# A fused decoder layer on one core: GpSimd places a step's queries ahead, TensorE turns the maxima alone

## The chip, the cores and the metric

The kernel runs on one core of one Trainium2 chip. The metric is the device time of one execution in microseconds (us). The profile calls the engines PE (TensorE matmuls), PEld (TensorE weight loads), DVE (VectorE), ACT (ScalarE), POOL (GpSimd) and SP (SyncE, whose queue issues the DMAs here).

## What is computed

The reference is one decoder layer on x of shape (8, 128, 128), that is 8 batch entries of 128 tokens of width 128. It has three parts, each on the layer norm of x and added back to x:

```python
x = x + attn(layernorm(x), ...)      # self attention, 16 heads of 8, scores * tau + delta, softmax
x = x + xattn(layernorm(x), ctx)     # cross attention, 16 heads of 8, masked, softmax
x = x + ffn(layernorm(x), ...)       # 64 experts, top 4 of 8 groups, top 8 experts, and a shared one
# in both attentions
scores = einsum('bhqd,bhkd->bhqk', Q, K) / sqrt(8)
attn   = softmax(scores);  out = einsum('bhqk,bhkd->bhqd', attn, V)
```

## The kernel before

The kernel is one program with its engines' instruction streams written out by hand; semaphores order them. After a start-up that makes queries and keys (to about 43 us of the profile) come 16 attention steps, s = 0 to 15: one batch entry each, the first 8 of the self attention (n = 0), the last 8 of the cross attention (n = 1). Then the experts' part runs in units to the end.

Queries and keys are kept "stacked". `qst` holds, for each of G = 4 groups of 4 heads, a band of 32 rows for each head: 8 rows that take the maxima, then the parts of the head's query. `kst` is the same for the keys. `scores(s, g)` on PE multiplies `qst` with the diagonal blocks of keys `kbd` (four matmuls in a step, one for each group; with a mask matmul before each from s = 8 on). DVE takes the row maxima of each (`maximum`, L1129), and `split_max` (L1136, L1137) writes them, as a high and a low part, to `negmax`.

`turn_max(s)` on PE then fills bank 5 with two matmuls: L521 copies the stacked queries of the step into it (identity times `qst`), and L524 adds the turned maxima. `queries_with_max(s)` copies the four bands of bank 5 to the four diagonal blocks of `qbd`, in the half `s % 2`: ACT two of them (L896), DVE the other two (L1145), 32 rows of 512 elements each. `scoresT(s, g)` on PE multiplies `kst` with `qbd`, which gives the transposed scores with the maximum taken off already; ACT takes the exponential (L887), `pv` multiplies with the values, `copy_o`, `turn_out`, `norm`, `turn_on`, `copy_on`, `project` and `add_residual` finish the step, each by its engine and partly one or two steps later.

In one round of the loop, PE runs `scores(s+1, 0)`, `turn_max(s)`, `scores(s+1, 1)`, `project(s-2)`, `pv(s-1)` with `scores(s+1, 2)` in its middle, `scoresT(s, 0)` and `(s, 1)`, `scores(s+1, 3)`, `turn_out(s-1)`, `scoresT(s, 2)` and `(s, 3)`, `turn_on(s-1)`. DVE runs `split_max(s)`, `maximum(s+1, 0)`, `queries_with_max(s)`, `maximum(s+1, 1)`, `add_residual(s-2)`, `maximum(s+1, 2)` and `(s+1, 3)`, `norm(s-1)`. In rounds 7 and 11 half of the cross attention's queries is made between: on ACT `queries_with_max(s)` and then the bias copy L942 to `qhl`, on DVE L1312, then the stacking matmuls on PE and the copies to `qst` by ACT (L922) and DVE (L1279, `second_stacked`); only after those can `scores(s+1, ...)` run. They need the layer norm of the first or last four entries, `second_inputs`, at the end of rounds 6 and 10. In rounds 2 and 3 `values(1, c)` of the cross attention are made as well.

POOL has little to do in these steps: after memsets it scales the values (L1421), makes `sel` (L1426, L1427) after step 0, and runs `normalise` (L263 to L277: some 15 tiny linked operations, then four of 128x128 into `xn`) and `add_bias` (L283) for each half, when `stats_ready` says that the residuals of its four entries are done. It then splits the first three expert weights (L1451 to L1455, L1444), normalises the first half for the experts (last `xn` at 154 us) and goes on to `low_inputs(0)` (L1437) and the second half. A POOL operation that is given to `link` is followed by a wait for its own completion.

Of the kernel before, what the change touches and what calls it, by code (L numbers as in the profile page):

```python
# [11 lines left out]
ALU = mybir.AluOpType  # L12
# [3 lines left out]
P = 128  # L16
B = 8
T = B * P
H, DK = 16, 8
G = 4  # L20
J = H // G
HALF = T // 2
E, I = 64, 64
# [5 lines left out]
STEPS = 2 * B  # L29
S_HI, S_MID, S_LO = 2 * G, 2 * G + DK, 2 * G + 2 * DK  # L30
PER_HALF = PAIRS + 1
UNITS = 2 * PER_HALF
LAG = 3
# [25 lines left out]
def decoder_layer(nc, x, ctxT, mask, pack_a, pack_b, w3, rowsd, outT):  # L59
# [3 lines left out]
    with ExitStack() as ctx:  # L63
# [3 lines left out]
        def sem(name):  # L67
            return ctx.enter_context(nc.semaphore(name))

        bank = [ctx.enter_context(nc.psum_tensor(f"bank{i}", [P, 512], F32)) for i in range(8)]  # L70
# [3 lines left out]
        SPREAD = 2 * FIRST - 2  # L74
# [3 lines left out]
        Bw = lambda name: pb[:, cols_b[name][0]:cols_b[name][1]]  # L78
        ident = A("ident")
# [10 lines left out]
        identr = sb("identr", [P, P], F32R)  # L90
# [21 lines left out]
        qst = sb("qst", [P, G, B, P], F32R)  # L112
# [3 lines left out]
        qbd = sb("qbd", [P, 2, G, J, P], F32R)  # L116
# [80 lines left out]
        k_stacked = sem("k_stacked")  # L197
        qst_ready = sem("qst_ready")
        qst_odd = sem("qst_odd")
        kst_ready = sem("kst_ready")  # L200
        kbd_ready = [sem(f"kbd_ready{i}") for i in range(2)]
        picks_ready = sem("picks_ready")
# [77 lines left out]
        def add_bias(eng, bias, lo, hi, done):  # L280

            eng.wait_ge(xn_ready, done)
            eng.tensor_tensor(xres[:, lo:hi, :], xres[:, lo:hi, :],  # L283
                              bias.unsqueeze(1).broadcast_to([P, hi - lo, P]), ALU.add).then_inc(bias_added, 1)

        def wait(eng, signal, value):

            if not isinstance(value, int) or value > 0:
                eng.wait_ge(signal, value)
# [95 lines left out]
        def _(pe):  # L385
# [130 lines left out]
            def turn_max(s):  # L516

                wait(pe, qbd_high, s)
                wait(pe, qbd_ready, s)
                wait(pe, qst_odd, {8: 2, 12: 4}.get(s, 0))  # L520
                pe.matmul(bank[5][:, :], identr[:, :], qst[:, :, s % B, :], start=True, stop=False,  # L521
                          skip_group_check=True)
                pe.wait_ge(max_split, s + 1)
                pe.matmul(bank[5][:, :].rearrange("p (g t) -> p g t", g=G), negmax[:, :],  # L524
                          identr[:, :].unsqueeze(1).broadcast_to([P, G, P]), start=False, stop=True,
                          skip_group_check=True).then_inc(max_turned, 1)

            def scoresT(s, g):
                n, b = s // B, s % B
# [256 lines left out]
        def _(act):  # L786
# [103 lines left out]
            def queries_with_max(s):  # L890

                act.wait_ge(max_turned, s + 1)
                wait(act, scoredT, G * (s - 1))
                for j in range(2):
                    r = slice(32 * j, 32 * j + 32)
                    last = act.activation(qbd[r, s % 2, :, j, :], bank[5][r, :].rearrange("p (g t) -> p g t", g=G),  # L896
                                          ACT.Copy)
                last.then_inc(qbd_high, 1)
# [119 lines left out]
        def _(dve):  # L1018
# [120 lines left out]

            def queries_with_max(s):  # L1140
                dve.wait_ge(max_turned, s + 1)
                wait(dve, scoredT, G * (s - 1))
                for j in range(2, J):
                    r = slice(32 * j, 32 * j + 32)
                    last = dve.tensor_copy(qbd[r, s % 2, :, j, :], bank[5][r, :].rearrange("p (g t) -> p g t", g=G))  # L1145
                last.then_inc(qbd_ready, 1)

# [247 lines left out]
        def _(pool):  # L1395
# [13 lines left out]
            for g in range(1, GE):  # L1409
# [5 lines left out]

            link, steps = chain(pool, pool_step)

            pool.wait_ge(delta_ready, 2)
            pool.wait_ge(v_copied, 2)
            v0 = vs[0][:, :, :, :].rearrange("p b h d -> p (b h) d")  # L1420
            pool.tensor_tensor(v0, v0, edelta[:, :, :].rearrange("p b h -> p (b h)").unsqueeze(2)  # L1421
                               .broadcast_to([P, B * H, DK + 1]), ALU.mult).then_inc(values_scaled, 1)
            pool.wait_ge(exped, G)
            pool.wait_ge(qbd_ready, 1)
            pool.wait_ge(bias_added, 1)
            link(pool.tensor_tensor(i2[:, :], ident[:, 0:E], ident[:, E:2 * E], ALU.add))  # L1426
            pool.tensor_copy(sel[:, :, :], i2[:, 0:SPREAD].unsqueeze(2).broadcast_to([P, SPREAD, I])).then_inc(sel_ready, 1)  # L1427

            pool.wait_ge(ld_b, 16)
            for c in range(2):  # L1430
                normalise(pool, link, 1, 4 * c, 4 * c + 4, False)
                add_bias(pool, Bw("bo"), 4 * c, 4 * c + 4, B + 4 * c + 4)

            def low_inputs(c):
                pool.wait_ge(xhi_ready, c + 1)
# [8 lines left out]
                pool.tensor_tensor(wlod[:, k % 4, :], ring[:, k % RING, 2, :], whid[:, k % 4, :].bitcast(F32),  # L1444
                                   ALU.subtract).then_inc(wlod_ready, 1)


            pool.wait_ge(exped, G * B)
            for k in range(LAG):
                pool.wait_ge(ld_w[k], 16)  # L1450
                pool.tensor_copy(whigu[:, k, :, :], ring[:, k, 0:2, :]).then_inc(whigu_ready, 1)  # L1451
                pool.wait_ge(whigu_ready, k + 1)
                pool.tensor_tensor(wlogu[:, k, :, :], ring[:, k, 0:2, :], whigu[:, k, :, :].bitcast(F32),
                                   ALU.subtract).then_inc(wlogu_ready, 1)
                pool.tensor_copy(whid[:, k, :], ring[:, k, 2, :]).then_inc(whid_ready, 1)  # L1455
                low_down(0, k)
            normalise(pool, link, 2, 0, 4, False)
            low_inputs(0)
            normalise(pool, link, 2, 4, B, False)

# [64 lines left out]
```

## Time and profile before

| | |
|---|---|
| median of 3 runs | 342.3 us (338.91, 342.3, 342.77) |
| profiled execution, its own time | 338.21 us |
| its span in the profile | 336.3 us, 1.9 us less |
| attention steps in the span | from about 43 to 163 us |
| busy | PE 89%, DVE 85%, ACT 65%, POOL 51% |
| granted TensorE clock, mean | 0.98 |

Times inside the profile are counted from the start of the span. The busy share of PE is modelled, since matmuls overlap; in the chain of waits a matmul of 512 columns takes 0.23 us of the path, which is the distance from one start to the next.

### The profile page before, as it was taken

How to read it: one execution, taken by the hardware profiler on the slowest of the kernel's cores; microseconds unless marked ns; L12 is line 12 of the kernel's file. 1: busy time of each engine (PE TensorE's matmuls, PEld its weight loads, DVE VectorE, ACT ScalarE, POOL GpSimd, SP SyncE). 2: the span in 40 equal slices, each digit the busy share in tenths (PEclk: the TensorE clock that was granted, in tenths of full speed). 3: DMA queues.
4: the chain of work that ended last, by engine and by line, in shares of the span. 5: the costliest groups of instructions: out<-in, count | busy, mean ns of one | idle time of the engine just before them, and what ended most of it. 6: DMA issues, size and time to landing. Idle time of an engine off the chain costs nothing.

```text
span 336.3 us, 6408 instructions
## 1 busy us (share of the span) xinstructions
PE 299.2 (89%) x1705; PEld 206.3 (61%) x1705; DVE 285.0 (85%) x579; ACT 219.5 (65%) x458; POOL 173.0 (51%) x247
## 2 busy tenths in 40 slices
PE   0799959999998999999938987988999899999995
PEld 0634745666665566556625855756778677777773
DVE  4997796788878886887978799999998798899994
ACT  1296727768974667467517975566777577677773
POOL 9440020000350085044076786577888588888883
PEclk9999997999999999999969999799999999999999
DMA  7700021111311111210004756446662666776621
GB/s 285 236 1 0 9 55 31 25 40 33 63 34 32 32 41 25 42 23 2 2 0 126 218 169 217 138 153 197 195 197 79 223 203 216 224 220 218 217 91 62
DMA packets 30889, 36.80 MB, mean 109 GB/s; under 512 B 5136, under 2 KB 22288, under 8 KB 30736
## 3 DMA queue, kind: packets, MB, share of 16 engines
q1 hardware_dynamic: 30864, 36.51, 36.2%
q8 instruction: 11, 0.18, 0.2%
q14 instruction: 14, 0.11, 0.1%
HBM read 31.77 MB, written 0.79 MB: 97 GB/s over the span
## 4 chain that ended last, share of the span: by engine, by line
PE 41%; DVE 18%; POOL 18%; issue 12%; ACT 5%; DMA 4%; SPq 0%; POOLq 0%; DVEq 0%; ACTq 0%
PE bank L390 30%; POOL qbd L1467 11%; POOL kst L1444 5%; DVE conv L1360 2%; DMA conv<-coefficient_rows 2%; DVE kst L1166 2%; PE bank L512 2%; PE bank L537 2%; DVE rawmax L1129 2%; DMA xres<-x 1%; DVE qbd L1145 1%; PE bank L524 1%; PE bank L772 1%; DVE vs L1369 1%; POOL xn L277 1%
## 5 line engine op out<-in xcount | busy, mean ns | idle before, releaser
L390 PE MATMUL bank<-khl,kst 128*128 128x512 f32 x396 | 108.6, 410 | 15.2 <-DVE kst L1166 9.2
L1467 POOL TENSOR_TENSOR qbd<-vs,qbd 128x512 fp32r<-128x512 f32 x65 | 84.1, 1294 | 33.8 <-ACT qbd L1008 33.8
L390 PEld LDWEIGHTS bank<-khl,kst 128*128 128x128 f32 x396 | 71.8, 192 | 42.6 <-DVE kst L1166 18.3
L977 ACT ACTIVATE bank<-bank 128x512 f32<-128x512 f32 x63 | 36.7, 582 | 37.6 <-PE bank L390 37.6
L1129 DVE TENSOR_REDUCE rawmax<-bank 128x4 f32<-128x512 f32 x64 | 43.0, 683 | 12.7 <-PE bank L390 11.7
L1360 DVE TENSOR_TENSOR conv<-bank,conv 128x512 f32<-128x512 f32 x61 | 41.7, 684 | 8.3 <-DMA conv<-coefficient_rows 4.7
L1166 DVE TENSOR_TENSOR kst<-ring,kst 128x256 fp32r<-128x256 f32 x63 | 48.7, 773 | 0.0
L1369 DVE TENSOR_TENSOR vs<-conv,bank 128x512 f32<-128x512 f32 x66 | 45.3, 687 | 3.3
L1008 ACT ACTIVATE qbd<-vs 128x512 fp32r<-128x512 f32 x66 | 41.0, 622 | 7.3 <-DVE vs L1369 7.3
L263 POOL TENSOR_SCALAR nwt<-mv 128x4 f32<-128x4 f32 x4 | 0.9, 228 | 76.6 <-DVE mv L1023 76.6
L1444 POOL TENSOR_TENSOR kst<-ring,kst 128x128 fp32r<-128x128 f32 x64 | 39.2, 612 | 0.2
L887 ACT ACTIVATE conv<-bank 128x512 f32<-128x512 f32 x64 | 35.0, 597 | 5.8 <-PE bank L390 5.2
L390 PE MATMUL bank<-kbd,qst 128*128 128x512 f32 x64 | 32.4, 514 | 0.6 <-DVE rawmax L1129 0.6
L390 PE MATMUL bank<-qbd,kst 128*128 128x512 f32 x64 | 30.0, 520 | 0.3
L772 PE MATMUL bank<-qbd,kst 128*128 128x512 f32 x66 | 26.5, 401 | 0.8 <-DVE kst L1377 0.8
L773 PE MATMUL bank<-qbd,kst 128*128 128x512 f32 x66 | 26.0, 395 | 0.0
L774 PE MATMUL bank<-qbd,kst 128*128 128x512 f32 x66 | 26.0, 394 | 0.0
L914 ACT ACTIVATE kst<-ring 128x256 fp32r<-128x256 f32 x63 | 25.8, 410 | 0.0
L896 ACT ACTIVATE qbd<-bank 32x512 fp32r<-32x512 f32 x32 | 18.8, 587 | 10.3 <-PE bank L524 10.0
L1145 DVE CAST qbd<-bank 32x512 fp32r<-32x512 f32 x32 | 22.2, 693 | 2.8 <-PE bank L524 2.2
L875 ACT ACTIVATE oT<-bank 128x512 f32<-128x512 f32 x16 | 9.6, 598 | 16.0 <-PE bank L390 16.0
L390 PE MATMUL bank<-conv,vs 128*9 128x128 f32 x512 | 19.2, 274 | 0.0
(195 smaller groups left out, 501.3 us busy)
## 6 DMA issues: line engine op xcount, KB each, us to landing
conv<-coefficient_rows SPq DMA_DIRECT2D x122, 128.0 KB, 3.0
ring<-w SPq DMA_DIRECT2D x66, 192.0 KB, 2.9
kbd<-kst SPq DMA_DIRECT2D x60, 64.0 KB, 2.0
pa<-pack_a SPq DMA_DIRECT2D x1, 1140.0 KB, 6.5
xres<-x SPq DMA_DIRECT2D x1, 512.0 KB, 4.2
ctxs<-ctxT SPq DMA_DIRECT2D x1, 512.0 KB, 7.1
outT<-qc SPq DMA_DIRECT2D x2, 256.0 KB, 2.1
pb<-pack_b SPq DMA_DIRECT2D x1, 449.0 KB, 7.8
```

Source lines behind the costliest of these rows:

```text
L390: return pe.matmul(out, lhsT, rhs, start=start, stop=stop)
L772: pe.matmul(acc, whid[:, w, :], hhi[:, w, :], start=False, stop=False, skip_group_check=True)
L773: pe.matmul(acc, whid[:, w, :], hlo[:, w, :], start=False, stop=False, skip_group_check=True)
L887: act.activation(probs[:, i % 8, :, :].rearrange("p j t -> p (j t)"), bank[2 + i % 2][:, :], ACT.Exp, scale=SCALE).then_inc(exped, 1)
L977: act.activation(out, four(2 + p), ACT.Silu).then_inc(silu_done, 1)
L1008: act.activation(hhi[:, k % 4, :].rearrange("p (b t) -> p b t", b=4), hx[k % 4], ACT.Copy).then_inc(hhi_ready, 1)
L1129: dve.tensor_reduce(rawmax[:, s % 2, g, :].unsqueeze(2), bank[i % 2][:, :].rearrange("p (j k) -> p j k", j=J), AX.X, ALU.max, negate=True) ...
L1166: dve.tensor_tensor(wlogu[:, k % 4, :, :], ring[:, k % RING, 0:2, :], whigu[:, k % 4, :, :].bitcast(F32), ALU.subtract).then_inc(wlogu_rea ...
L1360: dve.tensor_tensor(out, gate, spread[:, k % ROWS, :, :], ALU.mult).then_inc(gate_scaled, 1)
L1369: dve.tensor_tensor(hx[k % 4], scaled[:, 4 * p:4 * p + 4, :], four(4 + p), ALU.mult).then_inc(h_done, 1)
L1444: pool.tensor_tensor(wlod[:, k % 4, :], ring[:, k % RING, 2, :], whid[:, k % 4, :].bitcast(F32), ALU.subtract).then_inc(wlod_ready, 1)
L1467: pool.tensor_tensor(hlo[:, k % 4, :].rearrange("p (b t) -> p b t", b=4), hx[k % 4], hhi[:, k % 4, :].bitcast(F32).rearrange("p (b t) -> p ...
```

## The change

Before a step's maxima are known, POOL copies the four bands of `qst` (32 rows of 4 x 128) into the diagonal blocks of `qbd` by `place_queries(s)`, with a link between them, and signals `q_placed`. PE leaves out L521. ACT and DVE copy only the 8 rows of maxima of each band and wait for `q_placed` in place of the `scoredT` wait, which moves to POOL. POOL's other work of the attention steps is interleaved with the copies in a fixed order: place 0, values scaled, place 1, place 2, place 3, `sel`, place 4 to 6, `normalise(1, 0..4)` and `add_bias`, place 7 to 10, `normalise(1, 4..8)` and `add_bias`, place 11, place 12, weights 0, place 13, weights 1, place 14, `normalise(2, 0..4)`, place 15, weights 2, then on as before.

```diff
@@ turn_max (PE)
                 wait(pe, qst_odd, {8: 2, 12: 4}.get(s, 0))
-                pe.matmul(bank[5][:, :], identr[:, :], qst[:, :, s % B, :], start=True, stop=False,
-                          skip_group_check=True)
                 pe.wait_ge(max_split, s + 1)
                 pe.matmul(bank[5][:, :].rearrange("p (g t) -> p g t", g=G), negmax[:, :],
-                          identr[:, :].unsqueeze(1).broadcast_to([P, G, P]), start=False, stop=True,
-                          skip_group_check=True).then_inc(max_turned, 1)
+                          identr[:, :].unsqueeze(1).broadcast_to([P, G, P]), start=True, stop=True).then_inc(max_turned, 1)
@@ queries_with_max (ACT; the same on DVE for j = 2, 3)
                 act.wait_ge(max_turned, s + 1)
-                wait(act, scoredT, G * (s - 1))
+                act.wait_ge(q_placed, s + 1)
                 for j in range(2):
-                    r = slice(32 * j, 32 * j + 32)
+                    r = slice(32 * j, 32 * j + S_HI)
@@ POOL
+            def place_queries(s):
+
+                n, b = s // B, s % B
+                if b % 4 == 0:
+                    pool.wait_ge(qst_ready, G * (b // 4 + 1) if n == 0 else 2 * G + 2 * (b // 4) + 2)
+                if n == 1 and b % 4 == 0:
+                    pool.wait_ge(qst_odd, 2 * (b // 4) + 2)
+                wait(pool, scoredT, G * (s - 1))
+                for j in range(J):
+                    r = slice(32 * j, 32 * j + 32)
+                    copied = pool.tensor_copy(qbd[r, s % 2, :, j, :], qst[r, :, b, :])
+                    if j < J - 1:
+                        link(copied)
+                copied.then_inc(q_placed, 1)
+                pool.wait_ge(q_placed, s + 1)
+
+            place_queries(0)
             pool.wait_ge(delta_ready, 2)
             ...
+            place_queries(1)
             ...
+            for s in range(2, STEPS):
+                place_queries(s)
+                if s == 3:
             ...
+                if s in (6, 10):
+                    c = s // 4 - 1
+                    normalise(pool, link, 1, 4 * c, 4 * c + 4, False)
+                    add_bias(pool, Bw("bo"), 4 * c, 4 * c + 4, B + 4 * c + 4)
+                if s in (12, 13):
+                    split_weights(s - 12)
+                if s == STEPS - 2:
+                    normalise(pool, link, 2, 0, 4, False)
+            split_weights(2)
             low_inputs(0)
             normalise(pool, link, 2, 4, B, False)
```

## Rows read from the trace of the kernel before

**Rows 1.** The page: busy time, share of the span and instructions of each engine.
```profile
PE 299.2 (89%) x1705; PEld 206.3 (61%) x1705; DVE 285.0 (85%) x579; ACT 219.5 (65%) x458; POOL 173.0 (51%) x247
```
**Rows 2.** Chain of waits, rounds 9 and 10: start us, us on the path, what.
```profile
113.42 0.23 PE bank L521
...
119.76 0.23 PE bank L521
```
**Rows 3.** Timeline of DVE, round 9: start, us, what, idle before and releaser.
```profile
112.70 0.19 DVE L1137 TENSOR_TENSOR negmax<-rawmax,negmax 128x16 fp32r<-128x16 f32 x1
...
114.18 1.40 DVE L1145 CAST qbd<-bank 32x512 fp32r<-32x512 f32 x2
```
**Rows 4.** Timeline of PE, rounds 9 and 3.
```profile
75.22 0.74 PE L390 MATMUL bank<-khl,pick 128*128 128x512 f32 x2 [0.35 <-DVE vs L1083]
...
116.17 0.39 PE L537 MATMUL bank<-identb,maskb 128*128 128x512 bf16 x1
```
**Rows 5.** Line L524: what its engine sat idle for before it (us, times).
```profile
  DVE negmax L1137: 8.2, 5
```
**Rows 6.** Tiles qbd and qst: duration ns min/median/max, first and last start.
```profile
L1145 DVE CAST qbd<-bank x32: 689/692/698, 50.8 to 156.7; 32x512 fp32r<-32x512 f32 x32
...
L1116 DVE CAST qst<-bank x4: 680/690/692, 36.3 to 39.0; 128x512 fp32r<-128x512 f32 x4
```
**Rows 7.** Groups of POOL by form: count | busy us, mean ns | idle before.
```profile
L1467 POOL TENSOR_TENSOR qbd<-vs,qbd 128x512 fp32r<-128x512 f32 x65 | 84.1, 1294 | 33.8 <-ACT qbd L1008 33.8
...
L1451 POOL CAST kst<-ring 128x256 fp32r<-128x256 f32 x3 | 1.2, 397 | 0.0
...
L1427 POOL CAST pa<-i 128x384 f16<-128x384 f32 x1 | 0.5, 503 | 0.1
```
**Rows 8.** Timeline of POOL, 47 to 155 us.
```profile
47.78 2.17 POOL L1421 TENSOR_TENSOR vs<-vs,edelta 128x1152 f32<-128x1152 f32 x1 [27.48 <-DVE vs L1083]
...
88.75 0.23 POOL L263 TENSOR_SCALAR nwt<-mv 128x4 f32<-128x4 f32 x1 [30.74 <-DVE mv L1023]
...
96.34 1.15 POOL L283 TENSOR_TENSOR xres<-xres,pb 128x512 f32<-128x512 f32 x1
...
124.72 1.09 POOL L283 TENSOR_TENSOR xres<-xres,pb 128x512 f32<-128x512 f32 x1
125.76 0.40 POOL L1451 CAST kst<-ring 128x256 fp32r<-128x256 f32 x1
...
151.04 3.14 POOL L277 TENSOR_SCALAR xn<-xres,mv,nwt 128x128 f32<-128x128 f32 x4
```
**Rows 9.** Timeline of ACT, rounds 7, 11 and 15.
```profile
97.33 1.17 ACT L896 ACTIVATE qbd<-bank 32x512 fp32r<-32x512 f32 x2
98.52 0.69 ACT L942 ACTIVATE qhl<-bank,pb 128x512 fp32r<-128x512 f32 x1
...
126.78 1.19 ACT L896 ACTIVATE qbd<-bank 32x512 fp32r<-32x512 f32 x2
...
156.58 1.19 ACT L896 ACTIVATE qbd<-bank 32x512 fp32r<-32x512 f32 x2
```
**Rows 10.** Timeline of DVE, rounds 0, 7, 8 and 10 to 11.
```profile
50.02 0.19 DVE L1137 TENSOR_TENSOR negmax<-rawmax,negmax 128x16 fp32r<-128x16 f32 x1
...
99.25 0.75 DVE L1312 SCALAR_TENSOR_TENSOR qhl<-bank,pb,qhl 128x512 fp32r<-128x512 f32 x1 [0.60 <-ACT qhl L942]
...
104.17 0.69 DVE L1279 CAST qst<-bank 128x512 fp32r<-128x512 f32 x1
...
106.58 0.18 DVE L1136 CAST negmax<-rawmax 128x16 fp32r<-128x16 f32 x1
...
125.18 0.67 DVE L1136 CAST negmax<-rawmax 128x16 fp32r<-128x16 f32 x1
125.88 0.31 DVE L1137 TENSOR_TENSOR negmax<-rawmax,negmax 128x16 fp32r<-128x16 f32 x1
```
**Rows 11.** Stretch 52 to 54 us: busy of each engine, then clock, DMA share, GB/s.
```profile
52.00:54.00 2.00, 1.56 (x4) 1.15 (x4) 1.52 (x3) 0.68 (x2) 0.00 (x0) 0.50 0.00 0
```

More of the change, by code:

```diff
@@ L199, in decoder_layer @@
         qst_odd = sem("qst_odd")
+        q_placed = sem("q_placed")
         kst_ready = sem("kst_ready")
@@ L1141, in queries_with_max @@
                 dve.wait_ge(max_turned, s + 1)
-                wait(dve, scoredT, G * (s - 1))
+                dve.wait_ge(q_placed, s + 1)
                 for j in range(2, J):
-                    r = slice(32 * j, 32 * j + 32)
+                    r = slice(32 * j, 32 * j + S_HI)
                     last = dve.tensor_copy(qbd[r, s % 2, :, j, :], bank[5][r, :].rearrange("p (g t) -> p g t", g=G))
@@ L1422, in _ @@
                                .broadcast_to([P, B * H, DK + 1]), ALU.mult).then_inc(values_scaled, 1)
[L1423 to L1432, printed above, removed]
+            place_queries(1)
             def low_inputs(c):
@@ L1445, in low_down, with split_weights @@
                                    ALU.subtract).then_inc(wlod_ready, 1)
-            pool.wait_ge(exped, G * B)
-            for k in range(LAG):
+            def split_weights(k):
+                pool.wait_ge(exped, G * B)
                 pool.wait_ge(ld_w[k], 16)
@@ L1456, in _ @@
                 low_down(0, k)
-            normalise(pool, link, 2, 0, 4, False)
+            pool.wait_ge(ld_b, 16)
+            for s in range(2, STEPS):
+                place_queries(s)
+                if s == 3:
+                    pool.wait_ge(exped, G)
+                    pool.wait_ge(qbd_ready, 1)
+                    pool.wait_ge(bias_added, 1)
+                    link(pool.tensor_tensor(i2[:, :], ident[:, 0:E], ident[:, E:2 * E], ALU.add))
+                    pool.tensor_copy(sel[:, :, :], i2[:, 0:SPREAD].unsqueeze(2).broadcast_to([P, SPREAD, I]))                        .then_inc(sel_ready, 1)
+                if s in (6, 10):
[7 more added lines that the diff above has]
+            split_weights(2)
             low_inputs(0)
```

## The prediction

> **What bounds the kernel now.** I read the page first: PE is busy 89% of the span and DVE 85%, POOL half [rows 1]. These are averages over a start-up, sixteen attention steps and the experts, and the change touches only the steps, so the next view is the chain of waits of a plain round. There the path stays on PE from one `turn_max` to the next: L521 stands in it at 113.42 and again at 119.76 [rows 2], a period of 6.34 us, and it takes 0.23 us each time. PE is the bound of these rounds. Last I read the timelines of the four engines round by round, since two kinds of round differ: in 2 and 3 PE waits for the values' copies on DVE (the row at 75.22) [rows 4], and in 7 and 11 the queries of the cross attention are made in a chain through POOL, ACT, DVE and PE. In that chain POOL is no idle engine: it starts `normalise` at 88.75, straight behind the last statistics, and its `xn` is what `second_inputs` waits for; `add_bias` follows at 96.34 [rows 8].
>
> **What is removed.** One matmul a step, 16 x 0.23 = 3.7 us of PE time at most. It counts where PE is back to back, and only up to the next thing that ends a wait. L524 sat idle five times for `negmax` [rows 5], in rounds 0, 7, 8, 11 and 12: there L521 ran inside the wait and removing it gives nothing. In 2 and 3 DVE's values are late, nothing again. In 5, 6, 10 and 14 what follows is a POOL chain that starts from statistics already taken; what PE gains after that start is given back at its end. That leaves rounds 1, 4, 9 and perhaps 13: I take three, -0.7 us. The cover in round 9 is enough: DVE's copies end at 114.18 + 1.40 = 115.58 [rows 3], `scoresT` starts at 116.17 [rows 4]; the 0.59 us shrink by 0.23.
>
> **The smaller copies.** ACT and DVE copy 8 rows instead of 32, with the same 512 elements in each row. A DVE copy of 512 elements takes 692 ns for 32 rows and 690 ns for 128 [rows 6], so the number of rows doesn't enter: zero. A gain would need a cost by rows, which these two rows exclude.
>
> **The new copies.** The trace has no POOL copy of 32x512. The nearest are casts of 256 elements in 397 ns and of 384 in 503 ns [rows 7], 0.106 us for 128 elements more, so 0.61 us for 512. Below it can't reach less than the 384 elements' 0.50 unless 32 rows are cheaper than 128; above stands the two-input operation of 512 elements, 1.29 us [rows 7]. I take 0.61, by the line through two operations of its own kind. Between linked operations POOL loses about 0.08 us (125.76 + 0.40 to the next start, as in the normalise sequence from L263 on). Four copies: 4 x 0.61 + 3 x 0.08 = 2.7 us (2.2 at 0.50, 5.4 at 1.29). In plain rounds they start when `scoresT(s-2, 3)` ends and are needed about a whole round of 6 us later, so they are hidden by more than 3 us. They aren't where POOL is late, because its queue is in order:
>
> Round 7. `place_queries(7)` stands behind `normalise` and `add_bias`, which end at 96.34 + 1.15 = 97.49 [rows 8]. The copies end at 97.45 + 2.7 = 100.15, and ACT's and DVE's copies, now at 97.33 and about the same [rows 9], start at 100.2: 2.9 us late. Queued behind them on ACT is L942 (98.52), behind that on DVE L1312 (99.25) [rows 9, 10], and then the stacking that `scores(8, ...)` waits for. Some slack lies between the exponentials and the copy to `qst` (about 0.4), so +2.5 us on the path (+2.0 with copies of 0.50, +5 with 1.29).
>
> Round 11. The same with `add_bias` ending at 125.8 [rows 8]: copies to 128.45, against ACT's start at 126.78 [rows 9], 1.7 late, +1.55 us. Before, the weights' split began at 125.76 and nobody waited for it; now it comes later, and its consumer, the experts' first unit, is past 160 us.
>
> Rounds 8 and 12. `place_queries(8)` waits for the last half of `qst`, whose copy ends at 104.17 + 0.69 = 104.86 [rows 10]. The four copies fill POOL to 107.6, just about when ACT and DVE would start (107.6). So the price is the one on `split_max` between: L1136 at 106.58. How these operations fare beside POOL two rows show: L1136 took 0.67 instead of 0.18 us while `add_bias` ran from 124.72, and ended at 125.85 with it; L1137 took 0.31 instead of 0.19 and ended with the next POOL cast [rows 8, 10]. Here L1136 would end with the third copy, at 106.95, and L1137 either slip in before the fourth (+0.2) or end with it (+0.7): 0.45 each, 0.9 us for both.
> The Trainium skill says so in SBUF — State Buffer, section Who interferes with whom: a DVE copy in a 2-port mode, or a DVE operation with two SBUF inputs against a GpSimd one that reads SBUF, takes a port pair shared with GpSimd as an exclusive lock, and the later one is blocked for the whole instruction. The rows at 125.18 and 125.88 agree; without the rule these two rounds would cost about 0.1 us each and the sum would be 0.7 less.
>
> Round 0. POOL's L1421 ends at 49.95 [rows 8] and `place_queries(1)` starts at once, beside L1137 at 50.02 [rows 10], which is on the path to L524: it ends with the first copy at 50.6 instead of 50.2, +0.4 us. `place_queries(0)` runs from about 39.8 and is done by 43.5, 7 us early.
>
> Round 5. `scoresT(4, 3)` ends and `split_max(5)` starts within 0.1 us of each other in the timelines, so L1137 meets the first copy: the 0.23 of this round's PE is lost and up to 0.5 more; +0.2 us.
>
> Round 15. `place_queries(15)` follows `normalise(2, 0..4)`, whose `xn` ends at 151.04 + 3.14 = 154.2 [rows 8], so it is done at 156.9, against ACT at 156.58 [rows 9] and DVE some 0.6 earlier: +0.35 us through ACT's part of the router.
>
> SP's queue is passed by nothing, and the experts' part is only shifted.
>
> **The sum.** -0.7 + 2.5 + 1.55 + 0.9 + 0.4 + 0.2 + 0.35 = +5.2 us. The profiled execution took 338.2 (span 336.3 and 1.9 around it) and would become 343.4. It lies 4.1 below the median of the runs, and I set the same difference on the median: 342.3 + 5.2 = 347.5 us. With copies of 0.50 us the sum is about +4, with 0.8 about +8.
>
> **Rivals.** (1) The delays shrink and PE's gain stays: if POOL's cost does depend on rows and 32 rows are a quarter of 128, the copies take 0.8 us in all, round 7 waits 1.0, round 11 none; +1.0 - 0.7 + 0.6 = about +1, 343.3 us, and with rounds 5 and 10 gaining too -1. For it: half of POOL idles. Against it: DVE shows no such thing [rows 6], and both POOL casts are of full height.
> (2) The side of slower. With `place_queries(7)` late PE stands still for 2 us in round 7, with 0.7 more before the stacking, and near that in round 11. After the 3.2 us of idle PE that ended at 50.26 the granted clock was 0.50 from 52 to 54 [rows 11], which is 1.2 GHz. If it falls here too, eight or nine matmuls at 0.46 instead of 0.23 cost 2 us a time: +9.2, 351.5 us. It decides once a pause draws the clock down; against it, the pauses are shorter and full rounds lie before them.
> (3) The meeting of `split_max` and POOL in the plain rounds. `split_max(9)` has its L1137 at 112.70 [rows 3], and `scoresT(8, 3)`, which would release POOL, ends at the same moment; DVE is first by some 0.05 us. If POOL comes first, L1137 ends with the first copy, 0.6 late, of which 0.2 was covered by L521: +0.4 in six rounds, +7.6, 349.9 us. The Trainium skill's rule above, that issue order decides who is blocked, is what this rests on.
>
> **How the numbers follow.** Forecast 0.55, (1) 0.12, (2) 0.18, (3) 0.12; 0.03 for a gain beyond all of them. The range goes from +1 less than (1) to (2) and a little more, 341.5 to 352.5; below it lies the better half of (1), above it long copies with a low clock. A difference under 2%, 6.8 us, is about what a measurement of this kernel can't tell from none. Slower by more takes in (2), (3) and the forecast with copies of 0.75 or more: 0.30. Faster by more would need a 6.8 us gain, nearly twice all of L521: 0.03. Within: 0.67.
>
> **What would show it.** In the profile after: no L521; POOL copies of 32x512 near 0.61 us, 64 of them; L896 and L1145 still at 0.59 and 0.69; ACT and DVE waiting for POOL in rounds 7 (near 3 us), 11 (1.7) and 15 (0.3 to 1), in no plain one; L1136 or L1137 stretched in rounds 0, 5, 8 and 12; period of round 9 down from 6.34 to 6.1 us. The prediction is wrong if the copies take under 0.3 or over 0.9 us, if the low clock shows near 100 us, or if the period of the plain rounds doesn't fall.

## The result and the profile after

The changed kernel takes 350.5 us, the median of 348.42, 350.08, 350.93 and a disturbed execution of 388.23 that the ratio leaves out; the kernel before took 340.6 in the same session, the median of four (338.91 to 342.77). The ratio is 1.027, 95% interval 1.016 to 1.037. A second comparison with more runs, told below, gives 350.1 against 341.8, ratio 1.0285, interval 1.0225 to 1.0344. The change costs 8 to 10 us. Forecast were 5.2 us more and 347.5 us.

The page of the changed kernel, busy times, against [rows 1]:

```profile
PE 303.2 (87%) x1689; PEld 208.1 (60%) x1689; DVE 288.4 (83%) x579; ACT 219.9 (63%) x458; POOL 211.9 (61%) x311
```

Sixteen matmuls are gone and 64 POOL operations have come, for 39 us of POOL's time. The tile `qbd`, duration min/median/max, against [rows 6]:

```profile
L1426 POOL CAST qbd<-qst x64: 599/607/849, 39.8 to 167.3; 32x512 fp32r<-32x512 f32 x64
...
L894 ACT ACTIVATE qbd<-bank x32: 569/588/590, 54.5 to 168.6; 8x512 fp32r<-8x512 f32 x32
L1143 DVE CAST qbd<-bank x32: 689/694/698, 54.5 to 168.7; 8x512 fp32r<-8x512 f32 x32
```

A POOL copy takes 0.607 us, the 0.61 that the line through two casts of 128 rows gave; ACT's and DVE's copies cost for 8 rows what they cost for 32 (0.588 and 0.692 before). So the prices were right, and what is left is who waits. Waits of the changed kernel, DVE's and ACT's: us in total, times, longest:

```profile
DVE qbd L1143 <- POOL qbd L1426: 7.7, 3, 3.6
```
```profile
ACT qbd L894 <- POOL qbd L1426: 5.6, 3, 2.7
```

Three times, no more: rounds 7, 11 and 15, as forecast. The timelines of round 7, POOL's first (start, us, idle before), against [rows 8]:

```profile
100.49 1.14 POOL L284 TENSOR_TENSOR xres<-xres,pb 128x512 f32<-128x512 f32 x1
101.58 2.61 POOL L1426 CAST qbd<-qst 32x512 fp32r<-32x512 f32 x4
```

ACT of the same stretch, against [rows 9]:

```profile
104.29 1.19 ACT L894 ACTIVATE qbd<-bank 8x512 fp32r<-8x512 f32 x2 [2.70 <-POOL qbd L1426]
105.50 0.69 ACT L940 ACTIVATE qhl<-bank,pb 128x512 fp32r<-128x512 f32 x1
```

And PE:

```profile
102.75 1.06 PE L391 MATMUL bank<-conv,vs 128*9 128x128 f32 x32
105.80 0.70 PE L391 MATMUL bank<-qbd,kst 128*128 128x512 f32 x2 [1.99 <-ACT qbd L894]
107.03 2.07 PE L391 MATMUL bank<-qhl,pick 128*128 128x512 f32 x4 [0.53 <-DVE qhl L1310]
```

The four copies start in the moment `add_bias` ends, ACT starts in the moment they end, and PE stands still for 1.99 us and again for 0.53. Then its next four matmuls take 2.07 us: the granted clock (the last number but two) has gone to 0.50, which is 1.2 GHz. Stretches of 2 us of the changed kernel, PE's busy time, clock, DMA share, GB/s:

```profile
102.00:104.00 2.00, 1.81 (x36) 1.00 0.12 23
104.00:106.00 2.00, 0.20 (x1) 1.00 0.00 0
106.00:108.00 2.00, 1.47 (x4) 0.72 0.00 0
108.00:110.00 2.00, 2.00 (x6) 0.50 0.00 0
110.00:112.00 2.00, 2.00 (x10) 0.93 0.00 0
```

The kernel before is at 1.00 in every stretch from 92 to 114 us. The splits of the maxima on DVE, of the rounds 8, 11 and 15, against [rows 10]:

```profile
114.49 0.48 DVE L1134 CAST negmax<-rawmax 128x16 fp32r<-128x16 f32 x1
115.01 0.63 DVE L1135 TENSOR_TENSOR negmax<-rawmax,negmax 128x16 fp32r<-128x16 f32 x1
...
133.44 0.17 DVE L1134 CAST negmax<-rawmax 128x16 fp32r<-128x16 f32 x1
133.65 0.99 DVE L1135 TENSOR_TENSOR negmax<-rawmax,negmax 128x16 fp32r<-128x16 f32 x1
...
165.39 0.57 DVE L1134 CAST negmax<-rawmax 128x16 fp32r<-128x16 f32 x1
166.00 0.63 DVE L1135 TENSOR_TENSOR negmax<-rawmax,negmax 128x16 fp32r<-128x16 f32 x1
```

What they meet on POOL (the timeline of the same kernel; the first row holds the four copies for step 8 and the first for step 9):

```profile
112.99 3.29 POOL L1426 CAST qbd<-qst 32x512 fp32r<-32x512 f32 x5 [8.79 <-DVE qst L1277]
...
133.51 1.09 POOL L284 TENSOR_TENSOR xres<-xres,pb 128x512 f32<-128x512 f32 x1
...
165.32 2.62 POOL L1426 CAST qbd<-qst 32x512 fp32r<-32x512 f32 x4
```

Undisturbed the two take 0.17 and 0.19. In round 8 the copies, 0.61 long with 0.06 between (four take 2.61), end at about 113.6, 114.3, 115.0 and 115.65: L1134 ends at 114.97 with the third, L1135 at 115.64 with the fourth. In round 11 it isn't a copy that L1135 meets but `add_bias`, and it ends at 134.64, 0.04 behind it.

To place the loss I use one measure for all kernels: the distance from one turn of the maxima (L524 before, L523 after) to the next, from the rows of PE's timelines. The kernels `before_again` and `after_again` are second profiles of the two kernels; the others are told below (`place_b_bias` is `place_before_bias`, `f_s_early` is `four_steps_early`). All numbers are us.

```
from round       0    1    2    3    4    5    6     7    8    9   10    11   12   13   14 | first turn, last turn to end
before_again  6.89 6.88 7.51 7.52 5.95 5.95 5.84 10.21 6.46 6.35 6.42 10.31 6.44 6.35 6.18 | 50.3  180.9
after         7.34 6.91 7.53 7.54 5.94 5.98 5.90 14.97 6.18 6.11 6.71 12.93 6.19 6.12 6.75 | 53.7  180.5
after_again   7.03 6.87 7.52 7.52 5.95 5.96 5.91 14.68 6.19 6.12 6.71 12.92 6.19 6.12 6.74 | 50.5  181.7
filled_pause  7.55 6.90 7.52 7.52 5.96 5.95 5.91 13.66 6.19 6.12 6.71 13.22 6.19 6.11 6.75 | 54.0  182.1
old_7_11      7.15 6.89 7.52 7.51 5.95 5.96 6.07 10.97 6.20 6.11 6.62 10.94 6.19 6.12 6.75 | 53.9  181.4
place_b_bias  7.47 6.87 7.52 7.53 5.95 5.97 6.23 12.00 6.19 6.12 6.74 11.62 6.20 6.12 6.75 | 53.8  184.0
copies_aside  7.36 6.88 7.53 7.52 5.95 5.95 5.85 10.97 6.45 6.35 6.72 10.95 6.45 6.35 6.20 | 53.7  179.1
matmul_back   7.84 6.86 7.53 7.52 5.94 5.98 5.82 14.80 6.45 6.35 6.72 12.39 6.45 6.34 6.20 | 53.8  181.9
plain_rounds  7.31 6.87 7.53 7.52 6.23 5.78 6.68 10.59 6.22 6.12 6.62 10.87 6.54 6.18 6.27 | 53.7  178.0
four_steps    7.74 6.89 7.53 7.51 5.98 5.96 5.86 10.21 6.21 6.12 6.66 10.20 6.21 6.12 6.19 | 51.7  179.8
f_s_early     7.74 6.88 7.52 7.52 5.93 5.97 5.86 10.86 6.21 6.11 6.66 10.87 6.22 6.11 6.18 | 51.5  180.6
```

I name a distance by the round it starts from. The matmul L521 in it is that of the next step, and so is the split of the maxima: the splits of steps 8, 11, 12 and 15 lie in the distances 7, 10, 11 and 14. In distances 1 to 5, where all kernels but `plain_rounds` agree, they repeat to 0.05 us, mostly to 0.02, so a difference of 0.1 can be read. The first turn, distance 0 and the way to the end don't repeat: they vary by 3.7, 0.95 and 6 us, also between kernels that do the same there (`four_steps` copies nothing on POOL before step 9 and has 7.74 in distance 0). The granted clock goes with it: behind the last turn it is at 0.50 for 3.4 us in `plain_rounds`, the shortest, and for 17 us in three stretches in `place_before_bias`, the longest. From the first turn to the last, `after_again` is 7.17 us longer than `before_again` (112.43 against 105.26): +4.47 in round 7, +2.61 in 11, +0.56 in 14, +0.29 in 10, +0.14 in round 0, +0.07 in 6, and -0.27, -0.23, -0.25, -0.23 in 8, 9, 12 and 13. Nearly all of the net sum lies in two rounds of sixteen.

### The profile page after: what moved, and what is told of

Read it like the earlier page. It is cut to its first block, busy times and chain, and to the rows that moved or that the text cites. A ratio compares the mean times of both kernels' runs of the same rounds, so it can differ in the third digit from the quotient of the medians.

```text
span 347.3 us, 6462 instructions
## 1 busy us (share of the span) xinstructions
PE 303.2 (87%) x1689; PEld 208.1 (60%) x1689; DVE 288.4 (83%) x579; ACT 219.9 (63%) x458; POOL 211.9 (61%) x311
## 4 chain that ended last, share of the span: by engine, by line
PE 36%; POOL 25%; DVE 17%; issue 13%; ACT 4%; DMA 3%; POOLq 0%; ACTq 0%; SPq 0%; DVEq 0%
PE bank L391 28%; POOL qbd L1490 13%; POOL kst L1450 6%; DVE qbd L1143 2%; DVE rawmax L1127 2%; POOL xn L278 2%; DVE conv L1358 1%; POOL qbd L1426 1%; DMA xres<-x 1%; PE bank L513 1%; DVE kst L1164 1%; PE bank L535 1%; DMA conv<-coefficient_rows 1%; PE bank L553 1%; PE bank L770 1%
## 5 line engine op out<-in xcount | busy, mean ns | idle before, releaser
L1426 POOL CAST qbd<-qst 32x512 fp32r<-32x512 f32 x64 | 39.2, 612 | 64.4 <-PE bank L391 25.0
L1164 DVE TENSOR_TENSOR kst<-ring,kst 128x256 fp32r<-128x256 f32 x63 | 49.5, 785 | 0.0
L391 PE MATMUL bank<-kbd,qst 128*128 128x512 f32 x64 | 34.2, 543 | 0.5 <-DVE rawmax L1127 0.5
L894 ACT ACTIVATE qbd<-bank 8x512 fp32r<-8x512 f32 x32 | 18.7, 585 | 19.4 <-PE bank L523 13.1
L1143 DVE CAST qbd<-bank 8x512 fp32r<-8x512 f32 x32 | 22.2, 693 | 8.6 <-POOL qbd L1426 7.7
L916 ACT ACTIVATE kst<-ring 128x128 fp32r<-128x128 f32 x63 | 19.0, 302 | 0.0
```

The costliest lines, as they stand in the source:

```text
L391: return pe.matmul(out, lhsT, rhs, start=start, stop=stop)
L1164: dve.tensor_tensor(wlogu[:, k % 4, :, :], ring[:, k % RING, 0:2, :], whigu[:, k % 4, :, :].bitcast(F32), ALU.subtract).then_inc(wlogu_rea ...
L1426: copied = pool.tensor_copy(qbd[r, s % 2, :, j, :], qst[r, :, b, :])
```

## Experiments

Theory: the forecast's mechanism, POOL's queue in rounds 7 and 11, with the low clock on top in round 7. Rivals: the low clock is most of it, in both rounds and at the start; the meeting of copies and splits is most of it, in the plain rounds too; the new matmul count is worth less than taken.

**Both kernels again (after_again, before_again).** No edit.

> The changed kernel once more, for the granted clock of several runs. Theory: of the 11.0 us by which its span is longer, some 3 us lie before step 0, where the granted clock was 0.50 from 42 to 48 us in the profile of after and 1.00 in that of before, although the two kernels run the same matmuls there; if this is chance, some of its runs show mean clocks near 0.97 and times near 347, others near 0.956 and 350, in steps of about 3 us. Rival: the fall belongs to the change (GpSimd's first copies from 39.8 us on), and every run has it: one level, near 350.

> The kernel before once more. By the theory of chance it has the same two levels, about 339 and 342.5 us, and a profile on the upper level shows the low clock between 42 and 48 us. By the rival its two levels have another cause and its profile never shows a low clock there.

Measured: 350.06 us (346.38 to 352.57), ratio 1.0285, interval 1.0225 to 1.0344; and 340.81 us for the kernel before, ratio 1.000 to the other runs of it (0.996 to 1.0045). The loss is real. The two levels that were expected can't be told apart: the times spread from 346.4 to 352.6 us for the changed kernel and from 338.4 to 342.6 for the kernel before. The profile of `before_again` is the fastest of its executions, so it can't say what the slower ones do at 42 to 48 us. The profile of `after_again` has no low clock there, where the profile of `after` has it, and its first turn of the maxima comes at 50.5 instead of 53.7. Stretches of the changed kernel, first profile:

```profile
42.00:44.00 2.00, 2.00 (x10) 0.50 0.51 103
44.00:46.00 2.00, 2.00 (x9) 0.50 0.02 4
46.00:48.00 2.00, 2.00 (x12) 0.50 0.00 0
```

and second:

```profile
42.00:44.00 2.00, 2.00 (x17) 1.00 0.49 98
44.00:46.00 2.00, 1.59 (x13) 1.00 0.00 0
46.00:48.00 2.00, 0.47 (x1) 1.00 0.32 66
...
102.00:104.00 2.00, 1.33 (x3) 0.68 0.00 0
104.00:106.00 2.00, 2.00 (x7) 0.50 0.00 0
```

The fall in round 7 is in both (the last two rows are round 7 of `after_again`), the fall at 42 us in one; `after_again` falls to 0.50 at 48.1 instead, until 54.9 us. Three us of the 11 between the first two profiles (347.3 against 336.3) are therefore this start.

**Matmuls in the pause (filled_pause).** Nine unused matmuls a time on PE in rounds 7 and 11, where it would stand still; their result goes nowhere.

```diff
                 later(s, 1)
+                if making is not None:
+                    for _ in range(FILL):         # FILL = 9
+                        mm(bank[0][:, :], identr[:, :], qst[:, :, 0, :])
                 if now:
```

> The changed kernel with nine matmuls of 512 columns (their result is not used) put ahead of scoresT in rounds 7 and 11, where TensorE stands still for 2 us and waits for the late copies. Theory: the low clock from 107 to 110 us follows from that pause and costs about 1.3 us; with the pause filled the granted clock stays 1.00 there, the distance from L523 of round 7 to that of round 8 falls from 14.97 to about 13.6 us, and the time by 1.3 us. Rival: the clock falls for another reason, or the fillers cost more than they keep: no change or up to 1 us more.

Measured: 350.1 us, ratio 1.0253 (1.0169 to 1.0338), which can't be told from the changed kernel: the 1.3 us that were expected in the time don't show there. The distances decide. In the profile:

```profile
104.00:106.00 2.00, 2.00 (x20) 1.00 0.00 0
106.00:108.00 2.00, 1.55 (x7) 1.00 0.00 0
108.00:110.00 2.00, 1.96 (x11) 1.00 0.00 0
```

The clock stays at 1.00 and round 7 takes 13.66 us instead of 14.68 and 14.97; in round 11, where the clock never fell, the fillers cost 0.30 (13.22 against 12.92). So the low clock is worth 1.0 to 1.3 us, in round 7 alone, and up to 0.3 more if the fillers cost there what they cost in 11.

**Steps 7 and 11 as before (old_7_11).** In these two PE, ACT and DVE do what the kernel before does, and POOL copies nothing.

```diff
+OLD = (7, 11)
@@ turn_max: if s in OLD the matmul of the queries is put back
@@ queries_with_max (ACT and DVE)
-                act.wait_ge(q_placed, s + 1)
+                if s in OLD: wait(act, scoredT, G * (s - 1))
+                else: act.wait_ge(q_placed, PLACED(s))
-                    r = slice(32 * j, 32 * j + S_HI)
+                    r = slice(32 * j, 32 * j + (32 if s in OLD else S_HI))
@@ place_queries: if s in OLD: return
```

> The changed kernel, but steps 7 and 11 as before (matmul of the queries, full copies by ScalarE and VectorE, no copies on GpSimd). Theory: these two late placements are most of the loss; round 7 goes back from 14.97 to about 10.9 us (10.2 plus the blocked split of the maxima in round 8) and round 11 from 12.93 to about 11.2, together 5.5 to 6 us faster than the changed kernel. Rival: the rounds are long because of the placement for steps 8 and 12 and the blocked split, and only about 2 us come back.

Measured: 345.0 us, ratio 1.0134 (1.0056 to 1.0212): 5.1 us of the 8 to 10 are back with two steps of sixteen (5.7 in the two distances). Round 7 takes 10.97 and round 11 10.94. What is left of their loss, 0.76 and 0.63, is the copies for steps 8 and 12 meeting the splits; DVE of this kernel, round 8:

```profile
110.72 0.39 DVE L1143 CAST negmax<-rawmax 128x16 fp32r<-128x16 f32 x1
111.14 0.64 DVE L1144 TENSOR_TENSOR negmax<-rawmax,negmax 128x16 fp32r<-128x16 f32 x1
```

**The copies ahead of add_bias (place_before_bias).** All steps changed; only the order on POOL in rounds 6 and 10 differs.

```diff
             for s in range(2, STEPS):
-                place_queries(s)
+                if s not in (7, 11):
+                    place_queries(s)
...
                     normalise(pool, link, 1, 4 * c, 4 * c + 4, False)
+                    place_queries(s + 1)
                     add_bias(pool, Bw("bo"), 4 * c, 4 * c + 4, B + 4 * c + 4)
```

> The changed kernel with the copies of steps 7 and 11 moved ahead of add_bias in GpSimd's queue. Theory of the queue: the copies of ScalarE and VectorE in rounds 7 and 11 start 1.1 us earlier each, so the time falls by 2.2 us, and by up to 1.2 more if the shorter pause of round 7 leaves the clock at 1.00. Rival: the late operation is the copies' own wait for scoredT or qst, not the queue, and nothing changes; or the split of the maxima meets the copies instead of add_bias and gives part back.

Measured: 347.44 us, ratio 1.0138 (1.0066 to 1.021). Round 7 takes 12.00 us, 2.7 less than in `after_again`, round 11 11.62, 1.3 less, round 6 0.32 more, since the split of step 7 now meets the copies (its L1135 takes 0.51). `add_bias` takes 1.1 us, so bringing the copies forward by it saves 1.5 us more than itself in round 7. PE stands still for 0.75 and 0.53 us there instead of 1.98 and 0.47, and the clock stays at 1.00: the low clock goes away with the longer pause. The repair is worth some 3 us between the first turn and the last (2.6 by the medians, which are of two sessions), and it still loses to the kernel before.

**The copies without their readers (copies_aside).** POOL makes the same copies at the same places of its queue, but into a tile of its own that nobody reads; PE, ACT and DVE do in all steps what the kernel before does, and none waits for POOL.

```diff
+        aside = sb("aside", [P, G, P], F32R)
@@ place_queries; PE, ACT and DVE as with OLD = all steps
-                    copied = pool.tensor_copy(qbd[r, s % 2, :, j, :], qst[r, :, b, :])
+                    copied = pool.tensor_copy(aside[r, :, :], qst[r, :, b, :])
```

> The kernel before in what TensorE, ScalarE and VectorE do, but with GpSimd's queue of the changed kernel, its copies going to a scratch tile that nobody waits for. This leaves what GpSimd does to the others by its ports and by doing its old work later: the splits of the maxima of rounds 0, 8, 11, 12 and 15 are blocked as in the changed kernel and the sigmoids of the router by low_inputs. Theory: +0.3, +0.9, +0.3, +0.9, +0.3 and +0.7, 3 to 3.5 us slower than before. Rival: nearly all the loss is the wait for q_placed, and this kernel is within 1 us of before.

Measured: 344.25 us against 340.87, from four executions between 339.62 and 346.97, too far apart to decide on 3 us. The distances decide. 8, 9, 12 and 13 are as before. Distance 7 is 10.97, +0.76, with nobody waiting for the copies, 11 +0.64, 10 +0.30, 14 +0.02, together 1.7 us. (Distance 0 has +0.47, with the low clock at the start.) So the meetings are about a quarter of the 7.17 us, more than the rival had and less than the theory. DVE of this kernel, round 8:

```profile
110.48 0.48 DVE L1144 CAST negmax<-rawmax 128x16 fp32r<-128x16 f32 x1
111.00 0.64 DVE L1145 TENSOR_TENSOR negmax<-rawmax,negmax 128x16 fp32r<-128x16 f32 x1
```

So copies that no instruction waits for stretch the two splits to the same 0.48 and 0.64 as in the changed kernel: the price is the meeting itself. The Trainium skill's rule of SBUF — State Buffer, section Who interferes with whom, that the later of the two stays blocked for the whole instruction, agrees with these rows. `after_again` less this kernel is 3.71 in round 7, 1.97 in 11 and 0.54 in 14: what the waits for the copies and the missing matmul do together, which the next kernel takes apart. Round 7 of `filled_pause` less this kernel is 2.69: the late copies without the low clock, with up to 0.3 of the fillers in it.

**The queries' matmul back (matmul_back).** The changed kernel, but PE turns the queries again ahead of the maxima; ACT and DVE still copy 8 rows, so that result is unused.

```diff
+                pe.matmul(bank[5][:, :], identr[:, :], qst[:, :, s % B, :], start=True, stop=False,
+                          skip_group_check=True)
                 pe.wait_ge(max_split, s + 1)
...              (the turn of the maxima is added to it again: start=False)
```

> The changed kernel with the matmul of the queries put back in front of the turn of the maxima (ScalarE and VectorE still copy only the rows of maxima, so its result isn't used). Theory: the matmul counts only where TensorE is back to back with nothing else late, rounds 9, 10, 13 and 14, so putting it back costs 1.0 us against the changed kernel. Rival: it is worth 0.23 us in all sixteen, 3.7 us.

Measured: 350.04 us, ratio 1.0247 (1.018 to 1.0313). Distances 8, 9, 12 and 13 go back to 6.45, 6.35, 6.45 and 6.34: the matmuls of steps 9, 10, 13 and 14 are worth 0.22 to 0.26 each, 0.97 in all. But 11 is 0.53 shorter than in `after_again` and 14 is 0.54 shorter, so that from turn 8 to turn 15 the kernel with the matmul takes 50.90 us and the one without it 50.99. POOL's chain of rounds 9 to 11 starts from statistics: without the matmul PE and DVE come 0.5 us earlier to round 11, and DVE waits 2.61 us for the copies instead of 2.07. Likewise the split of step 15 comes 0.5 earlier and meets one copy more (0.57 + 0.63 in the changed kernel); with the matmul back it is, on DVE,

```profile
166.16 0.17 DVE L1137 CAST negmax<-rawmax 128x16 fp32r<-128x16 f32 x1
166.37 0.58 DVE L1138 TENSOR_TENSOR negmax<-rawmax,negmax 128x16 fp32r<-128x16 f32 x1
```

In the changed kernel the matmul saved is thus worth nothing. In distances 1 to 5 its return costs nothing either (5.94 and 5.98 in 4 and 5, with it and without). The reason shows in round 5 of `after_again`, PE's timeline:

```profile
85.36 0.43 PE L523 MATMUL bank<-identr,negmax 128*128 128x512 f32 x1
85.63 0.39 PE L391 MATMUL bank<-kbd,qst 128*128 128x512 f32 x1
85.98 0.73 PE L391 MATMUL bank<-khl,pick 128*128 128x512 f32 x2
```

and ACT's:

```profile
85.24 0.69 ACT L825 ACTIVATE kst<-bank,key_rows 128x512 fp32r<-128x512 f32 x1
85.81 0.28 ACT L879 ACTIVATE onT<-bank 128x128 f32<-128x128 f32 x1
```

The matmul at 85.98 stacks the next keys in the bank that ACT's L825 is just emptying, and that copy ends at 85.93. PE, 0.23 earlier, waits there for ACT. Rounds 1 and 4 have such a pair too: ACT's copy ends at 58.18 and 79.99, the next stacking matmul starts at 58.24 and 80.03. From round 6 on no keys are stacked.

**Rounds 0, 7, 8, 11, 12 and 15 as before (plain_rounds).** The edit of old_7_11 with `OLD = (0, 7, 8, 11, 12, 15)`.

> The changed kernel with steps 0, 7, 8, 11, 12 and 15 as before, so that GpSimd places queries only for the ten steps in which it has a whole round for it. Theory: the delays of the queue and the blocked splits of the maxima go, except for step 1's copies beside the split of step 0 (+0.3 us); rounds 9, 10, 13 and 14 keep their 0.25 us each, rounds 1 to 6 keep nothing: about 0.7 us faster than before, 341.1 against 341.8. Rival: the removed matmul is worth 0.23 us in every plain round, 2 us faster than before; or GpSimd's work in the way costs what is gained, no change.

Measured: 341.7 us, ratio 0.9997 (0.9952 to 1.0042): no gain. Distances 8, 9 and 13 have it (6.22, 6.12 and 6.18), but where a step is left out, the copies for the next one start at another moment and meet other splits. Those of steps 8 and 12, which the expectation had free, take 0.39 + 0.64 and 0.38 + 0.64 beside the copies for 9 and 13; the second half of the split takes 0.51 in step 5, 0.48 in 13 and 0.65 in 15. DVE of this kernel in round 7:

```profile
100.31 0.17 DVE L1143 CAST negmax<-rawmax 128x16 fp32r<-128x16 f32 x1
100.51 1.05 DVE L1144 TENSOR_TENSOR negmax<-rawmax,negmax 128x16 fp32r<-128x16 f32 x1
```

Here it is `add_bias` that the split meets, 0.9 late; round 6 takes 6.68 instead of 5.84.

**Only the four rounds that gain (four_steps, four_steps_early).** POOL places the queries of steps 9, 10, 13 and 14; its other work is in the order of the kernel before. `four_steps` holds the copies for 9 and 13 until the split of the step ahead is done; `four_steps_early` doesn't.

```diff
+OLD = (0, 1, 2, 3, 4, 5, 6, 7, 8, 11, 12, 15)
@@ POOL
             for c in range(2):
                 normalise(pool, link, 1, 4 * c, 4 * c + 4, False)
                 add_bias(pool, Bw("bo"), 4 * c, 4 * c + 4, B + 4 * c + 4)
+                if c == 1:
+                    for k in range(LAG):
+                        split_weights(k)
+                for s in (9 + 4 * c, 10 + 4 * c):
+                    if s % 4 == 1:                    # four_steps alone
+                        pool.wait_ge(max_split, s)    # four_steps alone
+                    place_queries(s)
```

> POOL places the queries of steps 9, 10, 13 and 14 only; all other steps are as in the kernel before, and the copies of 9 and 13 are held until the split of step 8 and 12 is done. Theory (the gain is 0.25 us in each of the rounds 9, 10, 13 and 14, where PE sets the time, and the losses come from POOL's queue at steps 8, 12 and 15 and from VectorE's split meeting the copies): rounds 9, 10, 13 and 14 take 6.2, 6.1, 6.2 and 6.1 us between turns of the maxima (before: 6.46, 6.34, 6.45, 6.35), rounds 7 and 11 stay at 10.2 and 10.3, the end at 6.2; 1.0 us less in all, a ratio of 0.997, which an interval of some 0.005 on each side can hardly show, so the periods of the profile decide. Rival (the held copies come too late for step 9 and 13, or POOL's other work in these rounds is late behind them): round 8 or 12 grows by 0.3 us or more and the gain is gone. Rival (the matmul gain was never there by itself): 6.4 in all four.

> As four_steps, but without the hold: the copies for steps 9 and 13 start as soon as the stacked queries are there, and can run beside VectorE's split of steps 8 and 12. Theory (the split is blocked by the copies): the splits of steps 8 and 12 take 0.5 us and more instead of 0.2 and 0.3, and the distances into rounds 8 and 12 grow by 0.5 to 0.75 us each, so that 1.0 us gained becomes 0 to 0.3 lost: ratio 1.000. Rival (the split isn't touched, and all of the copies' cost was POOL's queue): as four_steps, 0.997, with rounds 7 and 11 at 10.2 and 10.3.

Measured: `four_steps` 340.16 us against 341.77, ratio 0.9968, interval 0.9931 to 1.0005; `four_steps_early` 341.21, 1.0028 (0.9983 to 1.0073). The distances: 6.21, 6.12, 6.21, 6.12 where the kernel before has 6.46, 6.35, 6.44, 6.35, and 10.21 and 10.20 in rounds 7 and 11 with the hold, 10.86 and 10.87 without. DVE in round 8 with the hold:

```profile
108.92 0.18 DVE L1143 CAST negmax<-rawmax 128x16 fp32r<-128x16 f32 x1
109.14 0.19 DVE L1144 TENSOR_TENSOR negmax<-rawmax,negmax 128x16 fp32r<-128x16 f32 x1
```

and without:

```profile
108.68 0.40 DVE L1143 CAST negmax<-rawmax 128x16 fp32r<-128x16 f32 x1
109.11 0.64 DVE L1144 TENSOR_TENSOR negmax<-rawmax,negmax 128x16 fp32r<-128x16 f32 x1
```

Holding POOL's copies by some 2 us (they start at 109.39 with the hold and at 107.09 without) is worth 0.65 us in each of the two rounds. From turn 8 to turn 14 `four_steps` is 0.81 us shorter than the kernel before, of the 0.94 of the four steps; distance 10 gives 0.24 back and round 11 takes 0.11. Over all fifteen distances it is 0.13 longer, since distance 0, where it does what the kernel before does, has 7.74 instead of 6.89 with the low clock of its start. Its interval reaches to 1.0005, so a gain in the whole time isn't shown: it is read in the distances alone.

## Why the prediction was right in kind and short in size

**The matmul: -0.7 forecast, about 0 measured.** It was to count in rounds 1, 4, 9 and perhaps 13. It counted for steps 9, 10, 13 and 14, 0.97 us, and rounds 11 and 14 gave back 0.53 and 0.54. Rounds 1 and 4 gained nothing, since I named PE as the bound of every plain round from a chain that shows two of them, 9 and 10 [rows 2], and didn't ask what PE's next operation waits for in the others. I also misread the five waits of L524 [rows 5]: they are rounds 0, 8, 11 and 12, with round 0 twice, once for its weight load on PEld; the turn of round 7 waits for nothing. That a gain ahead of a POOL chain is given back stood in the forecast, for 10 and 14; that the gain of round 9 goes the same way in 11 didn't.

**Smaller copies: 0.** Right, 0.588 and 0.694 us. **POOL's copies: 0.61 each, 2.7 for four.** Right, 0.607 and 2.61; the gap between two of them is 0.06, not 0.08. Rival (1), cheap copies, is out.

**Round 7: +2.5 forecast, +4.47 measured.** The queue's part was sized rightly: 3.71 over `copies_aside`, less 1.0 to 1.3 for the low clock, leaves 2.4 to 2.7. The rest is the clock, which the sum left out as a rival, and the split of step 8 (0.76).

**Round 11: +1.55 forecast, 1.44 measured** for the queue (12.39 in `matmul_back` less 10.95 in `copies_aside`); the other 0.53 are the matmul's gain given back, above, and 0.64 the split. The low clock doesn't come there, though PE waits too.

**Splits of rounds 8 and 12: 0.45 each forecast, 0.76 and 0.64 measured.** I let one of the two instructions be blocked and the other slip in or be blocked, and took the middle. Both were: in these rows a copy is always in flight, and each of the two instructions ends with a copy, the second with the one after.

**Round 0: +0.4 forecast, +0.33 measured in the split**: L1135 of `after_again` takes 0.52 beside the first copy, where 0.19 was the rule. Its first turn comes 0.17 later. The 0.14 in distance 0 can't be put down to the copies, since the clock is low there until 54.9 us and in `before_again` until 54.3. **Round 5: +0.2 forecast, 0.0 measured**; in neither profile is a split longer than 0.20 in rounds 1 to 6. The margin is thin: in `after_again` L1135 ends at 85.17 and the copies begin at 85.18. In `plain_rounds` POOL is first, L1144 takes 0.51 and distance 4 is 0.28 longer (distance 5 is 0.17 shorter), so the meeting that was forecast exists.

**Round 15: +0.35 forecast through ACT's wait for the copies; ACT waits 0.64.** It lies behind the last turn, where the distances end. There also a step of the router, L1190, takes 1.07 us instead of 0.26, while POOL runs `low_inputs` beside it. I hadn't looked at what POOL's later work would meet. Whether these 0.6 and 0.8 us reach the end can't be read, since the way from the last turn to the end varies more than that.

**Not in the sum at all:** distance 10, +0.29. The split of step 11 met `add_bias` before too (0.67 + 0.31) [rows 10], and what it meets behind `add_bias` is now a copy instead of a shorter cast of the weights: `copies_aside` has +0.30 there, 0.75 + 0.53, and `matmul_back` 0.74 + 0.53. In the changed kernel itself, where DVE is 0.5 earlier, the second instruction meets `add_bias` in its whole length (0.99), at the same price.

**The sum.** From the first turn to the last, with the terms as measured: matmul +0.09, queue in 7 with its clock 3.71, queue in 11 1.44, splits of 8 and 12 0.76 + 0.64, distance 10 0.30, distances 0 and 6 0.14 + 0.07, together +7.15 where `after_again` shows +7.17; before the first turn 0.17 more, behind the last up to 1.4. Forecast were 5.2 in all. Four terms make the gap: the low clock of round 7, 1.0 to 1.3, left out of the sum, is the largest; the others are the matmul's gain of 0.7, which is given back; the splits, 1.4 instead of 0.9; and distance 10, 0.3. Rival (2) came true in one of its two places at half its price; its chance of 0.18 was too low for round 7 and its 2 us were too much, since the clock is low for 3.4 us only. Its 351.5 us lies nearer to the 350.5 than the forecast does, but not for its reason. Rival (3) didn't come: in the plain rounds of the changed kernel DVE stays first.

**Signs and luck.** One of the signs that I had named for a wrong forecast came, the low clock near 100 us, and another came by half: the distances fell in 8, 9, 12 and 13 and not in 1 to 6. That 347.5 lies 3 us under the 350.5 is in part luck. It stands on a median of 342.3; on those of the two comparisons, 340.6 and 341.8, the same +5.2 gives 345.8 and 347.0. Of the difference the forecast has 5.2 of 8.3 to 9.9 us.

**What stays open.** The medians differ by 9.9 us in the first comparison and by 8.3 in the second, the profiles by 8.1 (`after_again` against `before_again`), and the distances explain 7.2 of it. The rest lies before the first turn and behind the last and isn't settled. The low clock at 42 to 48 us is in nine of the twelve profiles: `before`, `before_again` and `after_again` lack it. `plain_rounds`, whose POOL copies nothing before 53.0 us, has 0.50 from 42.0 to 48.8, and `four_steps`, which copies nothing before step 9, from 43.8 to 47.2, so the copies aren't needed for it. That the change makes it more frequent by another way is possible; no profile of the kernel before caught it, and it wasn't tried.

## What to carry to other kernels

Work moved to an engine that is half idle is hidden only where its queue is empty: look at the rounds in which that engine's own chain is awaited, and put the copies ahead of what nobody awaits, or leave those rounds alone. One matmul less on the bounding engine is worth its time only in rounds whose next operation waits for no third engine, here 4 of 16, and it stays only if no wait for another chain follows. And a gain ahead of a chain that starts elsewhere comes back as a longer wait. Where POOL and DVE work side by side, small DVE operations on the path, here the two of the split, end when a POOL operation ends, and holding POOL's back until they are done can be worth more than starting them early, here 0.65 us each time.

## What the runs showed of the chip

A pause of PE can cost twice. In round 7 PE stood still for 1.99 us and 0.53 us with two matmuls between, and the granted clock went from 1.00 to 0.50 for about 3.4 us; in round 11 it stood still too, in the row

```profile
138.77 0.38 PE L535 MATMUL bank<-identb,maskb 128*128 128x512 bf16 x1 [1.43 <-ACT qbd L894]
```

with 0.16 before the stacking, and the clock stayed at 1.00. It stayed at 1.00 in round 7 of `place_before_bias` too, with pauses of 0.75 and 0.53. The fall came in all three profiles with a pause of 1.98 or 1.99 us in round 7 (`after`, `after_again`, `matmul_back`). What decides between that and 1.43 us, these runs don't tell.

The first instruction of the split, 0.17 us undisturbed, took 1.78 and 1.81 at the start of the two kernels beside POOL's 2.17 us operation that scales the values [rows 8], and 0.38 to 0.57 beside a copy. The second, 0.19 undisturbed, took 0.48 to 0.65 beside a copy and 0.99 to 1.05 beside `add_bias`: the price of a meeting is what POOL's operation has left, not what DVE's would take.
